# Two LoRA splits and two weight merges change places in a one-core transformer block kernel

## The chip, the cores and the metric

The kernel runs on one core of a Trainium2 chip. The metric is the device time of one execution in microseconds. A core has five engines with a queue of instructions each: TensorE (PE in the profile, with its weight loads as PEld), VectorE (DVE), ScalarE (ACT), GpSimd (POOL) and SyncE (SP, here the queue that issues nearly all DMAs). They run side by side and wait for each other through semaphores; within an engine the order is the program's.

## The reference

B = 2 batches of S = 512 rows of D = 512 features, HID = 1376, LoRA rank R = 16, all in float32.

```
mod = silu(c) @ wmod            -> sa, ca, ga, sb, cb, gb   (six rows of 512 for each batch)
ga, gb: the sign times max(|.|, 0.25)
h = layernorm(x) * (1 + ca) + sa
x = x + ga * (h @ W'^T + bias)                W' = weight, 32x32 blocks whose mask sums to 0 cleared
h = layernorm(x) * (1 + cb) + sb
h1 = h @ (w1 + 2 B1 A1)^T ;  h3 = h @ (w3 + 2 B3 A3)^T
x = x + gb * ((silu(h1) * h3) @ (w2 + 2 B2 A2)^T)
```

(The reference adds the LoRA terms as separate products; the kernel merges them into the weights.)

## The kernel before, in words

**Precision by parts.** Every float32 product is made as three products of rounded halves: high x high, high x low, low x high. So each operand needs a "high" copy (ScalarE) and a "low" remainder (VectorE or GpSimd, value minus high).

**Attention stage, up to some 48 us.** `attend(b, k, m, tiles)` (L1342) adds feature chunk k of batch b into one PSUM bank for each of four row tiles. For batch 1, tiles 2 and 3 share their banks (acc[0], acc[1]) with tiles of batch 0, so `attend(1, 0, 0, last_two)` waits until VectorE's `attn_gate(0, i)` (L995) has read the bank. Behind the gates come the residual adds `add_x1` (tiles i = 0, 1 on GpSimd, L569; 2, 3 on VectorE, L1001), the layer-norm moments `moment_f` (VectorE, L843, L845), GpSimd's `root` (L525, L528) for the reciprocal deviations, `columns_f` (TensorE L1288 transposes the modulation rows, VectorE L921, L922 takes them out), `centres`, the normed tiles (ScalarE L744, VectorE L855), and TensorE's transposes `turn(q)` (L1199). The modulation rows of the second half are `mod_rows_f` (L1281), copied by ScalarE's `mod_evacuate`, behind which ScalarE makes the fourth tile's moment.

**LoRA parts.** The LoRA matrices come in five cuts. `lora_first` (GpSimd, cuts 0 and 1) or `lora_high` (ScalarE, cuts 2 to 4) writes the high copy, and `lora_part(n)` on VectorE (L982) turns it into rows that hold high or low parts, one scalar_tensor_tensor instruction for the cut (cut 1 has 640 columns, cut 2 has 1120), counted by `parts_ready`. TensorE's merge(0) waits for two of them, GpSimd's `spread(2)` (L562) for three. `spread(j)` makes the small masked copies b13 that the merges of weight tile j multiply by.

**Weights.** The hidden dimension has 11 tiles of up to 128. Each has three pieces: (j, 0) and (j, 1) are halves of w1 and w3, (j, 2) is w2. For each piece, in this order: a DMA into one of four slots of `raw`; TensorE's `merge` (the LoRA product, L1370 for the halves, L1375 for w2); VectorE's `merge` (raw + 2 x that, L1011); ScalarE's `weight_high` (L750); VectorE's `weight_low` (L1017), which also frees the slot.

**Feed-forward stage.** 22 steps s (11 for each batch). In step s TensorE makes h1 into bank up_a, then h3 into up_b: `up_high` (high and low weights by the high activations, L1388, 8 products) and `up_rest` (high weights by the low activations, L1397, 4 products). In between it makes the merges of the next tile (`pieces_up(s)`), and behind h3 the `down` products (L1414 to L1416) of the step before. VectorE and ScalarE: Silu of up_a (L808), g = up_b x that (L1136), g_hi (L818), g_lo (L1142). Step 0 is written out by hand: high products of both banks first, then the rests, as the low activations come late, and `gate_rows(1)` (L1303) at its end, which waits for the merge whose bank it takes. The order of every queue is written by hand, in the loops over s at L802 (ScalarE), L1116 (VectorE) and L1486 (TensorE) and the straight lines ahead of them.

Of the kernel before, what the change touches and what calls it, by code (L numbers as in the profile page):

```python
# [130 lines left out]
def build(nc, x, x_cols, mask, weight, bias, ffn, lora, c, wmod_ca, wmod_sa, wmod, identity, consts, out):  # L131
# [4 lines left out]
    with ExitStack() as ctx:  # L136
# [474 lines left out]
        def _(act):  # L611
# [135 lines left out]
            def weight_high(r):  # L747
                act.wait_ge(merged, r + 1)
                src, dst, _ = weight_parts(r)
                nc.scalar.activation(dst, src, ACT.Copy).then_inc(w_high_ready, 1)  # L750
# [50 lines left out]
            lora_high(2)  # L801
            for s in range(B * HT):  # L802
                w = WIDTH[s % HT]
                act.wait_ge(h1_out, s + 1)
                if s:

                    act.wait_ge(g_low_ready, s)
                nc.scalar.activation(g[0:w], up_a[0:w], ACT.Silu).then_inc(silu_ready, 1)  # L808
                for at in pieces_up(s):
                    weight_high(PIECE[at])  # L810
                if piece_mid(s):
                    weight_high(PIECE[piece_mid(s)])
                if s == 0:
                    gate_abs(1)
                elif s == HT:
                    gated_high(0)
                act.wait_ge(g_ready, s + 1)
                nc.scalar.activation(g_hi[s % 2][0:w], g[0:w], ACT.Copy).then_inc(g_high_ready, 1)  # L818
                for j in gated_at(s):
                    gated_high(j)  # L820
                if piece_late(s):
                    weight_high(PIECE[piece_late(s)])
                if s == 0:
                    lora_high(3)
                elif s == 1:
                    lora_high(4)
                if s in STEP_TURN:
                    modulate_tile(STEP_TURN[s])

        @block.vector  # L830
        def _(dve):
# [85 lines left out]
            def columns_f():  # L917

                dve.wait_ge(cols_out, 1)
                src = up_b[:, 0:HALF].rearrange("p (c v h b) -> p v h c b", c=2, v=2, h=2)  # L920
                nc.vector.tensor_copy(shift[:].rearrange("p (h c) b -> p h c b", h=2), src[:, 0, :, :, 0:B])  # L921
                nc.vector.tensor_scalar(one_plus[:].rearrange("p (h c) b -> p h c b", h=2), src[:, 1, :, :, 0:B],  # L922
                                        1.0, None, ALU.add).then_inc(cols_ready, 1)
# [50 lines left out]
            def lora_part(n):  # L974
                lo, hi = LORA_CUTS[n]
                keep = KEEP_A if n in LORA_A else KEEP_B
                if n < LORA_POOL:
                    dve.wait_ge(parts_high_by_pool, n + 1)
                else:
                    dve.wait_ge(parts_high_ready, n + 1 - LORA_POOL)  # L980
                dve.wait_ge(const_loaded, 16)
                nc.vector.scalar_tensor_tensor(parts[:, lo:hi], f32(parts[:, lo:hi]), const[:, keep:keep + 1],  # L982
                                               lora_place(n), ALU.mult, ALU.add).then_inc(parts_ready, 1)
# [97 lines left out]
            uv_split()  # L1081
            masked_weight_low(1, 3)
            x_low(1, 3)
            lora_part(1)

            dve.wait_ge(norm_rows_out, 1)
            nc.vector.memset(f32(norm_values(0)), 0.0).then_inc(norm_first_cleared, 1)
# [4 lines left out]
            def moment_f(i):  # L1092
                dve.wait_ge(*x1_done(i))
                moment(NORM_F[0], i, xt[:, 0, ORDER[i]])
# [3 lines left out]
            add_x1(0, 3)  # L1098
            moment_f(1)
            moment_f(2)  # L1100
            columns_f()
            centres()
            norm_parts(1)
# [6 lines left out]
            for q in range(KT):  # L1110
                if q in WHOLE_DVE:
                    whole(q)
                low(q)
            lora_part(2)
            attn_gate(1, 0)
            for s in range(B * HT):  # L1116
                w = WIDTH[s % HT]
                if s == 5:
                    for t in range(2, T):
                        norm(1, t, t)  # L1120
                for at in pieces_up(s):
                    merge(PIECE[at])
                if s == 1:
                    lora_part(3)
                for at in pieces_up(s):
                    weight_low(PIECE[at])
                if piece_mid(s):
                    merge(PIECE[piece_mid(s)])
                    lora_part(4)
                    weight_low(PIECE[piece_mid(s)])  # L1130
                if s == HT:
                    gate_weights(0)

                dve.wait_ge(silu_ready, s + 1)
                dve.wait_ge(h3_out, s + 1)
                nc.vector.tensor_tensor(g[0:w], up_b[0:w], g[0:w], ALU.mult).then_inc(g_ready, 1)  # L1136
                if s == 0:
                    gates_of(1)
                if piece_late(s):
                    merge(PIECE[piece_late(s)])  # L1140
                dve.wait_ge(g_high_ready, s + 1)
                nc.vector.tensor_tensor(g_lo[s % 2][0:w], g[0:w], f32(g_hi[s % 2][0:w]),  # L1142
                                        ALU.subtract).then_inc(g_low_ready, 1)
                if piece_late(s):
                    weight_low(PIECE[piece_late(s)])
                if s < 2:
                    for i in ((1,), (2, 3))[s]:
                        attn_gate(1, i)
                if s == 2:
                    for i in range(T):  # L1150
                        add_x1(1, i)
                elif s in (3, 4):
                    for t in (2 * s - 6, 2 * s - 5):
                        dve.wait_ge(x1_by_dve, T - len(X1_POOL) + ORDER.index(t) + 1)
                        moment(NORM_F[1], t, xt[:, 1, t])
                    if s == 4:
                        for t in range(2):
                            norm(1, t, t)
                if s == HT:
                    gated_low(0)  # L1160
                    for n in range(T):
                        down_end(n)
                for j in gated_at(s):
                    gate_weights(j)
                    gated_low(j)
# [4 lines left out]
        def _(pe):  # L1170
# [114 lines left out]
            def columns_f():  # L1285
                pe.wait_ge(mod_rows_ready, 1)
                for c in range(2):
                    last = nc.tensor.transpose(up_b[:, c * P:(c + 1) * P], mod_rows[:, c * P:(c + 1) * P], ident[:])  # L1288
                last.then_inc(cols_out, 1)
# [101 lines left out]
            def up_rest(s, n, dst, signal):  # L1391
                b, j = divmod(s, HT)
                w = WIDTH[j]
                for k in range(KT):
                    if s == 0:
                        pe.wait_ge(low_by_dve, k + 1)
                    last = nc.tensor.matmul(dst[0:w], up_hi[j][:, k, n], ht_lo[b][:, k],  # L1397
                                            start=False, stop=(k == KT - 1))
                last.then_inc(signal, 1)
# [71 lines left out]
                attend(1, 1, m, last_two)  # L1471
            attend(1, 2, 0, last_two)
            columns_f()
            pe.wait_ge(parts_ready, 2)
            merge(0)
            for m in range(1, 3):
                attend(1, 2, m, last_two)
            attend(1, 3, 0, last_two)
            merge(1)
            attend(1, 3, 1, last_two)  # L1480
# [5 lines left out]
            for s in range(B * HT):  # L1486
                if s == HT:

                    pe.wait_ge(high_ready, KT + T)
                    pe.wait_ge(low_by_pool, T)  # L1490

                pe.wait_ge(*((silu_ready, s) if s else h_done(0)))
                if s:
                    up(s, 0, up_a, h1_out)
                else:

                    up_high(0, 0, up_a)

                    pe.wait_ge(*h_done(1))
                    up_high(0, 1, up_b)  # L1500
                    up_rest(0, 0, up_a, h1_out)
                for at in pieces_up(s):
                    merge(PIECE[at])
                if s == 2:

                    for t in range(T):
                        down(0, t)
                    merge(PIECE[piece_mid(s)])
                if s:

                    pe.wait_ge(g_ready, s)
                    up(s, 1, up_b, h3_out)
                else:
                    up_rest(0, 1, up_b, h3_out)
                if s == 0:
                    gate_rows(1)
                elif s == 1:
                    merge(PIECE[piece_late(s)])
                else:
                    for t in range(T):  # L1520
                        down(s - 1, t)
                        if t == 1 and piece_late(s):
                            merge(PIECE[piece_late(s)])
                if s in STEP_TURN:
                    turn_tile(STEP_TURN[s])
# [87 lines left out]
```

## Time and profile before

| | |
|---|---|
| median of 3 runs | 248.74 us (248.71 to 249.12) |
| the profiled execution's own time | 248.83 us |
| its span, first to last instruction | 247.0 us |
| busy: TensorE, its weight loads | 239.6 us (97%), 186.9 us (76%) |
| busy: VectorE, ScalarE, GpSimd | 150.1 (61%), 93.8 (38%), 41.9 us (17%) |
| granted TensorE clock | 0.999 of full speed |
| DMA | 26.38 MB, some 400 GB/s from 6 to 43 us, little after |

Times are from the start of the span. An engine's row gives the start and length of an instruction, or of several alike in one row (x4); the next instruction of VectorE starts some 0.08 us before the end of the one ahead of it, so what an instruction costs its queue is the distance of two starts. TensorE's products overlap more: one of 128x512 shows 0.39 us and is followed by the next after about 0.23. "[0.73 <-DVE wa L995]" is idle time ahead of the row and what ended it. A share of busy time says little here: it is an average over a first stage in which all engines have work and a second one in which TensorE is nearly alone.

### The profile page before, as it was taken

Reading aid. Unit: us, or ns where it says so; the run is one execution under the profiler, and the core shown is the slowest. Engines: PE = TensorE matmul, PEld = TensorE weight load, DVE = VectorE, ACT = ScalarE, POOL = GpSimd, SP = SyncE. Lnnn points to the kernel's source line nnn. Section 1 sums busy time; section 2 is a strip of 40 time slices with the busy share of each in tenths; the row PEclk is TensorE's granted clock in tenths of the full one; section 3 lists DMA queues with packets and bytes.
Section 4 is the critical chain, followed back from the end, with each engine's and each line's share of the span. In section 5 each row is a group of like instructions: output and inputs, shape, how many; then the busy total and the mean of one; then the engine's idle time right before and its main releaser. Section 6 shows DMA issues by size and latency. Waiting matters only on the chain.

```text
span 247.0 us, 3419 instructions
## 1 busy us (share of the span) xinstructions
PE 239.6 (97%) x1201; PEld 186.9 (76%) x1201; DVE 150.1 (61%) x262; ACT 93.8 (38%) x173; POOL 41.9 (17%) x57
## 2 busy tenths in 40 slices
PE   7999989999999999999999999999999999999993
PEld 5567556677778888888888778888888888888772
DVE  2779798989979768755555514745354245424524
ACT  2364495957443231647456212113121212122210
POOL 2002686311101034033032000440000000000000
PEclk9999999999999999999999999999999999999999
DMA  5999999702331231331234650030000000000005
GB/s 139 339 399 390 387 406 391 200 24 85 106 134 60 87 127 44 98 115 44 89 101 80 42 37 0 25 145 3 0 1 0 0 3 0 0 0 0 3 0 170
DMA packets 14565, 26.38 MB, mean 107 GB/s; under 512 B 1618, under 2 KB 3538, under 8 KB 14420
## 3 DMA queue, kind: packets, MB, share of 16 engines
q1 hardware_dynamic: 14112, 26.01, 34.5%
q8 instruction: 10, 0.16, 0.3%
q10 hardware_dynamic: 436, 0.15, 0.2%
q14 instruction: 7, 0.06, 0.1%
HBM read 23.27 MB, written 2.10 MB: 103 GB/s over the span
## 4 chain that ended last, share of the span: by engine, by line
PE 84%; DVE 7%; DMA 2%; issue 2%; ACT 2%; POOL 1%; SPq 0%; DVEq 0%; POOLq 0%; ACTq 0%
PE up_a L1388 17%; PE up_b L1388 16%; PE acc L1414 8%; PE up_a L1397 8%; PE acc L1416 8%; PE acc L1415 8%; PE up_b L1397 8%; PE acc L1342 3%; DMA wa<-in_weight 2%; PE side L1370 2%; PE side L1342 2%; DVE wa_lo L944 1%; DVE xt L1041 1%; DVE stats L843 1%; PE side L1375 1%
## 5 line engine op out<-in xcount | busy, mean ns | idle before, releaser
L1136 DVE TENSOR_TENSOR g<-up_b,g 128x512 f32<-128x512 f32 (+1 forms) x22 | 15.2, 690 | 43.2 <-PE up_b L1397 43.2
L1414 PE MATMUL acc<-w_hi,g_hi 128*128 128x512 f32 (+1 forms) x88 | 35.0, 397 | 0.0
L1416 PE MATMUL acc<-w_hi,g_lo 128*128 128x512 f32 (+1 forms) x88 | 34.8, 395 | 0.0
L1415 PE MATMUL acc<-w_lo,g_hi 128*128 128x512 f32 (+1 forms) x88 | 34.8, 395 | 0.0
L818 ACT ACTIVATE g_hi<-g 128x512 fp32r<-128x512 f32 (+1 forms) x22 | 13.9, 632 | 51.6 <-DVE g L1136 51.6
L1011 DVE SCALAR_TENSOR_TENSOR raw<-side,raw 128x512 f32<-128x512 f32 (+2 forms) x31 | 20.2, 677 | 19.1 <-PE side L1370 11.4
L750 ACT ACTIVATE w_hi<-raw 128x512 fp32r<-128x512 f32 (+2 forms) x33 | 20.3, 626 | 17.1 <-DVE raw L1011 17.0
L808 ACT ACTIVATE g<-up_a 128x512 f32<-128x512 f32 (+1 forms) x22 | 13.1, 596 | 32.6 <-PE up_a L1397 32.6
L1388 PE MATMUL up_a<-ht_hi,w_hi 128*128 128x512 f32 (+1 forms) x88 | 24.7, 401 | 0.3 <-ACT w_hi L750 0.3
L1388 PE MATMUL up_b<-ht_hi,w_hi 128*128 128x512 f32 (+1 forms) x88 | 23.9, 393 | 0.0
L1397 PE MATMUL up_b<-ht_lo,w_hi 128*128 128x512 f32 (+1 forms) x88 | 23.8, 392 | 0.0
L1397 PE MATMUL up_a<-ht_lo,w_hi 128*128 128x512 f32 (+1 forms) x88 | 23.8, 392 | 0.0
L1388 PE MATMUL up_a<-ht_hi,w_lo 128*128 128x512 f32 (+1 forms) x88 | 23.8, 392 | 0.0
L1388 PE MATMUL up_b<-ht_hi,w_lo 128*128 128x512 f32 (+1 forms) x88 | 23.7, 391 | 0.0
L1017 DVE TENSOR_TENSOR w_lo<-raw,w_hi 128x512 fp32r<-128x512 f32 (+2 forms) x33 | 21.6, 680 | 1.8
L1142 DVE TENSOR_TENSOR g_lo<-g,g_hi 128x512 fp32r<-128x512 f32 (+1 forms) x22 | 15.1, 688 | 8.1 <-ACT g_hi L818 7.9
L1414 PEld LDWEIGHTS acc<-w_hi,g_hi 128*128 128x128 f32 (+1 forms) x88 | 16.6, 188 | 4.4 <-issue 0.6
L562 POOL TENSOR_SCALAR b<-parts,half_on 128x128 fp32r<-128x128 f32 (+1 forms) x22 | 14.7, 678 | 29.9 <-PE side L1370 29.2
L1416 PEld LDWEIGHTS acc<-w_hi,g_lo 128*128 128x128 f32 (+1 forms) x88 | 16.6, 188 | 4.0
L1415 PEld LDWEIGHTS acc<-w_lo,g_hi 128*128 128x128 f32 (+1 forms) x88 | 16.6, 188 | 3.8
L1388 PEld LDWEIGHTS up_a<-ht_hi,w_lo 128*128 128x128 f32 (+1 forms) x88 | 16.3, 186 | 4.1
L1388 PEld LDWEIGHTS up_a<-ht_hi,w_hi 128*128 128x128 f32 (+1 forms) x88 | 15.9, 186 | 4.5 <-issue 0.5
(167 smaller groups left out, 340.8 us busy)
## 6 DMA issues: line engine op xcount, KB each, us to landing
raw<-in_ffn SPq DMA_DIRECT2D x33, 256.0 KB, 2.6
xt<-in_x SPq DMA_DIRECT2D x8, 256.0 KB, 10.8
wmod_sb<-in_wmod SPq DMA_DIRECT2D x2, 1024.0 KB, 15.3
wmod_sb<-in_wmod SPq DMA_DIRECT2D x1, 2048.0 KB, 14.5
out<-xt SPq DMA_DIRECT2D x8, 256.0 KB, 2.5
mask_sb<-in_mask SPq DMA_DIRECT2D x4, 256.0 KB, 7.1
ca_sb<-in_wmod_ca SPq DMA_DIRECT2D x4, 256.0 KB, 6.5
wa<-in_weight SPq DMA_DIRECT2D x4, 256.0 KB, 7.3
```

The source lines that it names most:

```text
L562: nc.gpsimd.tensor_scalar(b13[:, n, 0:w], f32(parts[:, LORA_B13 + j * P:LORA_B13 + j * P + w]), half_on[:, n:n + 1], None, ALU.mult).then_ ...
L750: nc.scalar.activation(dst, src, ACT.Copy).then_inc(w_high_ready, 1)
L818: nc.scalar.activation(g_hi[s % 2][0:w], g[0:w], ACT.Copy).then_inc(g_high_ready, 1)
L1011: nc.vector.scalar_tensor_tensor(w, merge_bank(r)[0:rows, 0:cols], SCALING, w, ALU.mult, ALU.add).then_inc(merged, 1)
L1017: nc.vector.tensor_tensor(low_part, src, f32(high), ALU.subtract).then_inc(w_ready, 1)
L1136: nc.vector.tensor_tensor(g[0:w], up_b[0:w], g[0:w], ALU.mult).then_inc(g_ready, 1)
L1142: nc.vector.tensor_tensor(g_lo[s % 2][0:w], g[0:w], f32(g_hi[s % 2][0:w]), ALU.subtract).then_inc(g_low_ready, 1)
L1388: nc.tensor.matmul(dst[0:w], w_part[j][:, k, n], ht_hi[b][:, k], start=(m == 0 and k == 0), stop=False)
L1397: last = nc.tensor.matmul(dst[0:w], up_hi[j][:, k, n], ht_lo[b][:, k], start=False, stop=(k == KT - 1))
L1414: nc.tensor.matmul(acc[t][:], hi, down_hi[j][0:w], start=(j == 0), stop=False)
L1415: nc.tensor.matmul(acc[t][:], hi, down_lo[j][0:w], start=False, stop=False)
L1416: last = nc.tensor.matmul(acc[t][:], lo, down_hi[j][0:w], start=False, stop=(j == HT - 1))
```

## The change

On VectorE, lora_part(1) moves from ahead of the four gates of batch 0 to behind the third tile's moments. lora_part(2) moves from behind the low activations to behind the merges of step 0, ahead of the low parts of the same pieces. On ScalarE the high part of piece (1, 0) is made ahead of step 0's Silu. On TensorE four attention products move ahead of merge(0) and its wait, and the merges of weight tile 1 move ahead of the rest of h1 in step 0. No instruction is added or removed.

```diff
@@ ScalarE, step loop
             for s in range(B * HT):
                 w = WIDTH[s % HT]
+                if s == 0:
+
+                    weight_high(PIECE[1, 0])
                 act.wait_ge(h1_out, s + 1)
...
                 for at in pieces_up(s):
-                    weight_high(PIECE[at])
+                    if at != (1, 0):
+                        weight_high(PIECE[at])
@@ VectorE
             masked_weight_low(1, 3)
             x_low(1, 3)
-            lora_part(1)
 
             dve.wait_ge(norm_rows_out, 1)
...
             moment_f(1)
             moment_f(2)
+            lora_part(1)
             columns_f()
...
                 low(q)
-            lora_part(2)
             attn_gate(1, 0)
             for s in range(B * HT):
...
                 for at in pieces_up(s):
                     merge(PIECE[at])
-                if s == 1:
-                    lora_part(3)
+                if s < 2:
+                    lora_part(2 + s)
                 for at in pieces_up(s):
                     weight_low(PIECE[at])
@@ TensorE
             columns_f()
+            for m in range(1, 3):
+                attend(1, 2, m, last_two)
             pe.wait_ge(parts_ready, 2)
             merge(0)
-            for m in range(1, 3):
-                attend(1, 2, m, last_two)
             attend(1, 3, 0, last_two)
...
                     pe.wait_ge(*h_done(1))
                     up_high(0, 1, up_b)
-                    up_rest(0, 0, up_a, h1_out)
                 for at in pieces_up(s):
                     merge(PIECE[at])
+                if s == 0:
+                    up_rest(0, 0, up_a, h1_out)
```

## Rows read from the trace of the kernel before

**Rows 1.** The page, section 4: shares of the chain that ended last, by engine.

```profile
PE 84%; DVE 7%; DMA 2%; issue 2%; ACT 2%; POOL 1%; SPq 0%; DVEq 0%; POOLq 0%; ACTq 0%
```

**Rows 2.** Table of stretches: from:to us, length, busy us (instructions) of each engine.

```profile
65.00:100.00 35.00, 34.97 (x159) 28.45 (x158) 28.90 (x50) 12.31 (x21) 7.22 (x12) 1.00 0.29 91
```

**Rows 3.** Timeline of TensorE, 34 to 67 us: start, length, what [idle before].

```profile
34.71 0.62 PE L1342 MATMUL acc<-wa_hi,ht_lo 128*128 128x512 f32 x2
36.07 1.06 PE L1342 MATMUL acc<-wa_hi,ht_hi 128*128 128x512 f32 x2 [0.73 <-DVE wa L995]
...
53.49 0.63 PE L1370 MATMUL side<-b,parts 128*128 128x256 f32 x4
...
55.23 1.08 PE L1303 MATMUL side<-wmod_sb,silu_c 128*32 128x128 f32 x32 [0.17 <-DVE raw L1011]
56.58 1.17 PE L1388 MATMUL up_a<-ht_hi,w_hi 128*128 128x512 f32 x4 [0.27 <-ACT w_hi L750]
...
59.42 0.64 PE L1370 MATMUL side<-b,parts 128*128 128x256 f32 x4
...
66.31 0.48 PE L1414 MATMUL acc<-w_hi,g_hi 128*128 128x512 f32 x1
```

**Rows 4.** Timeline of VectorE, 34 to 45 us.

```profile
34.34 0.90 DVE L982 SCALAR_TENSOR_TENSOR parts<-parts,const,lora_raw 128x640 fp32r<-128x640 f32 x1
35.20 1.37 DVE L995 SCALAR_TENSOR_TENSOR wa<-acc,rstd,mask_sb 128x512 f32<-128x512 f32 x2
...
37.82 1.28 DVE L1001 TENSOR_TENSOR xt<-wa,xt 128x512 f32<-128x512 f32 x1
...
39.83 0.66 DVE L1001 TENSOR_TENSOR xt<-wa,xt 128x512 f32<-128x512 f32 x1
...
42.71 0.17 DVE L921 COPY shift<-up_b 128x8 f32<-128x8 f32 x1 [0.59 <-PE up_b L1288]
...
43.63 0.68 DVE L1011 SCALAR_TENSOR_TENSOR raw<-up_a,raw 128x512 f32<-128x512 f32 x1
44.44 1.06 DVE L855 TENSOR_SCALAR work<-xt,moments,rstd 128x512 f32<-128x512 f32 x2
```

**Rows 5.** Timeline of GpSimd, 33 to 56 us.

```profile
33.45 2.27 POOL L562 TENSOR_SCALAR b<-parts,half_on 128x128 fp32r<-128x128 f32 x2 [0.40 <-PE up_b L1315]
36.01 2.54 POOL L569 TENSOR_TENSOR xt<-wa,xt 128x512 f32<-128x512 f32 x2 [0.29 <-DVE wa L995]
...
41.87 0.71 POOL L528 TENSOR_TENSOR rstd<-rstd,exponent 128x2 f32<-128x2 f32 x1
...
43.69 0.71 POOL L528 TENSOR_TENSOR rstd<-rstd,exponent 128x2 f32<-128x2 f32 x1
...
54.32 1.18 POOL L562 TENSOR_SCALAR b<-parts,half_on 128x128 fp32r<-128x128 f32 x2 [8.09 <-PE side L1370]
```

**Rows 6.** Timeline of VectorE, 51 to 67 us.

```profile
51.57 0.69 DVE L886 TENSOR_TENSOR ht_lo<-hbuf,ht_hi 128x512 fp32r<-128x512 f32 x1 [0.37 <-ACT hbuf L723]
52.53 1.38 DVE L982 SCALAR_TENSOR_TENSOR parts<-parts,const,ca_sb 128x1120 fp32r<-128x1120 f32 x1 [0.27 <-ACT parts L759]
...
54.49 1.28 DVE L1011 SCALAR_TENSOR_TENSOR raw<-side,raw 128x512 f32<-128x512 f32 x2
55.87 1.29 DVE L1017 TENSOR_TENSOR w_lo<-raw,w_hi 128x512 fp32r<-128x512 f32 x2
57.08 0.68 DVE L1136 TENSOR_TENSOR g<-up_b,g 128x512 f32<-128x512 f32 x1
...
59.93 1.29 DVE L1011 SCALAR_TENSOR_TENSOR raw<-side,raw 128x512 f32<-128x512 f32 x2
...
65.52 0.68 DVE L1017 TENSOR_TENSOR w_lo<-raw,w_hi 128x512 fp32r<-128x512 f32 x1
```

**Rows 7.** Timeline of ScalarE, 55 to 57 us.

```profile
55.21 1.23 ACT L750 ACTIVATE w_hi<-raw 128x512 fp32r<-128x512 f32 x2 [0.92 <-DVE raw L1011]
```

**Rows 8.** DMA issues at 23.2 us: out<-in, count, KB, us from issue to landing.

```profile
wmod_sb<-in_wmod SPq DMA_DIRECT2D x1, 2048.0 KB, 14.5
```

## The prediction

> **What bounds the kernel now.** The chain of waits comes first: 84% of the span on it is TensorE, 7% VectorE [rows 1]. The table of stretches then says where TensorE can still gain: from 65 to 100 us it works 34.97 of 35.00 us [rows 2], and it stays as dense to the end, so nothing behind 65 us gives anything by itself, while each microsecond by which TensorE reaches that point earlier comes off the end. So I read the timeline of each engine from 33 to 67 us. TensorE is held there in four places that bear on the change. Ahead of 36.07 us it waits for VectorE's first attention gate; issue stood at 34.71 + 2 x 0.237 = 35.18 [rows 3] (0.237 us is the pace of one product of 512 columns: twelve lie between 56.58 and 59.42). At 45 us its transposes wait for the two normed tiles that VectorE starts at 44.44 [rows 4]. Ahead of the gate rows at 55.23 it waits for a merge on VectorE, ahead of 56.58 for ScalarE's high part of the second weight tile [rows 3]: the four merge products of 53.49 and the four of the rest behind them would be issued by 54.91, so 0.3 us are lost there, and about 0.3 us again behind the gate rows. VectorE itself is full from 43.63 to 66 us, with gaps of 0.37, 0.27 and less [rows 4, 6], so both engines have to come earlier, or one holds the other.
>
> **First part: lora_part(1) behind the moments.** At 34.34 VectorE starts lora_part(1), and at 35.20 the memset and gate 0: 0.86 us in front of the gates [rows 4]. What else the gates need (the last attention products, the copy of the gate row) is there by 34.3, so I take the four gates 0.86 us earlier, and TensorE's 36.07 at 35.2, directly behind its 34.71 group. TensorE's next outside limit is the 2 MB of modulation weights: issued at 23.19 and landed 14.5 us later, at 37.7 [rows 8], against a new need at about 38.0. It just fits, and another 0.1 us here would not matter, because VectorE and not TensorE sets the next step.
>
> On VectorE the 0.86 us do not all survive. The add at 37.82 takes 1.28 us where the same form at 39.83 takes 0.66; it ends 0.55 us behind GpSimd's second add, which ends at 38.55 [rows 4, 5]. So this add goes by GpSimd. GpSimd is busy until 35.72 with the two spreads at 33.45, which take 2.27 us where the pair at 54.32 takes 1.18 [rows 5]; the second of them ran beside lora_part(1). Without that neighbour I let it end at about 35.3; then the two adds of 2.54 us end at 37.9, VectorE's add at 38.45 and everything up to the third moment 0.65 us earlier than before, at 41.47. If the spread stays as long as it is, the adds end at 38.3 and only 0.26 us survive.
>
> The Trainium skill (SBUF — State Buffer, Who interferes with whom) says that VectorE and GpSimd lock one port pair for a whole instruction, and that a VectorE instruction contends with a reading GpSimd one only with two SBUF inputs. By that rule the gates (one input in PSUM) leave the spread alone, and the 1.28 us of the add are a lock, in which the trace agrees; it would give the 0.65, not the 0.26.
>
> Now lora_part(1) itself runs, from 41.39 for 0.86 us, to 42.25. Before, VectorE sat idle 0.59 us ahead of 42.71, waiting for TensorE's columns [rows 4]; these now come at 41.85. So columns_f starts at about 42.2, 0.5 us earlier: the move pays with a gap that was empty. merge(0) follows 0.92 us later (42.71 to 43.63), at 43.12. TensorE's side of it, now behind four attention products and the wait for parts, is issued at about 42.55 and usable 0.51 us later (59.42 to 59.93 in the later merge [rows 3, 6]), at 43.06: level, no new stall. The four products moved ahead cost nothing, they are the same work in another order. Then the norm starts at 43.12 + 0.61 = 43.73, if the reciprocal deviations are there: GpSimd's last root ends at 44.40 now [rows 5] and hangs on ScalarE's moment behind TensorE's modulation rows, so it comes at 43.55. Before it was 44.44. I take **0.65 us** for this part. Bounds: up, the whole 0.86. Down: with 0.26 us, the norm at 44.1, 0.3 us gained. Lower still if lora_part(1) meets GpSimd's root at 41.87 (41.2 now), 0.71 us long [rows 5], and is held to its end: together with the 0.26 that is columns_f at about 43.1, a norm at 44.65, 0.2 us lost. The nearest row speaks against: the add at 39.83 ran its plain 0.66 us beside such a root.
>
> **Second part: the merges of weight tile 1 ahead of the rests, lora_part(2) behind them.** I work in the old clock, as if the first part did nothing. TensorE removes nothing; the four products at 53.49 [rows 3] move in front of the four of the h1 rest, and are issued four products earlier (4 x 0.23), at 52.57. Their banks are free by then (ScalarE's and VectorE's reads end at 51.5). Their results are usable at 53.08. VectorE frees itself from the last low part (51.57, 0.69) at 52.18 [rows 6]. Its sequence was: 0.35 us waiting for ScalarE's copy, lora_part(2) 1.30 (52.53 to 53.83), gate 0.66, two merges 1.3, 0.09 idle, two low parts 1.21, g at 57.08 [rows 6]. Now: gate 0.66 to 52.84, 0.24 us waiting for the merge, merges 1.21 to 54.29, lora_part(2) 1.30 to 55.59, low parts 1.21 to 56.80. So g comes 0.28 us earlier. ScalarE: high part of piece (1,0) from 53.8, Silu behind it at 54.35 (its input, behind the moved merges, is ready at 54.1), high part (1,1) done at 55.5, against 56.44 now [rows 7]. TensorE: rests to 54.9, gate rows without a wait to 55.9, step 1 at 55.95 instead of 56.58. Four products later it needs the low parts: at 56.9, and they end at 56.86, so it is held 0.1 us. Its merges of step 1 come at 58.87 instead of 59.42, and VectorE, which waited some 0.2 us for them at 59.93 [rows 6], starts them at 59.44. From there to the low part at 65.52 its order is the old one, 0.49 us earlier; TensorE's down product of 66.31 follows that low part (end 66.20) within 0.1 us [rows 3, 6]. So VectorE, not the 0.63 us that TensorE has gained, sets it: **0.5 us**. Bounds: up 0.63. Down: GpSimd's next spreads (54.32, 1.18 us [rows 5]) wait for the merge and for lora_part(2), so they now start at about 55.7, beside the two low parts, instead of beside merges. One spread of 0.6 let in ahead of a low part makes it -0.1, both make it -0.7. The row at 33.45 is the nearest: there GpSimd was the one stretched, so I keep the 0.5. The same page's lock would make either engine wait here, by which comes first; VectorE's queue is the fuller one. The spreads themselves have until 58.9 before TensorE wants them, 2 us of slack. Silu behind a high part costs nothing, as g waits for VectorE anyway. No DMA moves: the weight loads hang on the low parts, all earlier or at most as late.
>
> **Sum.** 0.65 + 0.50 = 1.15 us off the profiled execution's own 248.83 (span 247.03 and 1.8 around it), which is 0.09 above the median 248.74: 247.7 us. All that is gained at 66 us is carried, as TensorE does not wait behind it.
>
> **Rivals.**
> (a) Only the first part pays; a spread gets in between VectorE's low parts and the step-1 start is again held. For it: VectorE has no gap up to 66 us. 248.83 - 0.65 + 0.1 = 248.3.
> (b) Only the second pays; lora_part(1) meets GpSimd's root, columns_f stays at 42.7 to 43.1, the normed tiles where they were. Against: the add at 39.83. 248.83 - 0.5 + 0 to 0.2 = 248.3 to 248.5.
> (c) Neither: 248.8. The move of lora_part(2) only swaps one VectorE item for another, which is true of its sum; what counts is 0.28 us of idle time and the 0.2 at 59.93.
> (d) Slower: both spreads win against both low parts. They then end at 56.86 + 1.2 = 58.1, where TensorE wants them at 56.9 and had them in time for 57.59 before; 0.7 us lost there. With the first part at -0.2 to 0.3 this is 249.1 to 249.7. It decides from 0.55 us of hold on: below that the second part still gains. A pair of spreads did once take 2.27 us, but VectorE's own instructions around it were not longer.
>
> **Numbers.** Forecast (own range 247.2 to 248.2) 0.55; (a) 0.16; (b) 0.13; (c) 0.08; (d) 0.08. What a measurement can tell is about 0.5 us, so faster means below 248.24. Faster: 0.55 and half of (a) and a third of (b), some 0.68. Slower: (d), 0.08, of which a little stays within; with a little for what I don't see 0.08. Same: 0.24. The range reaches from both upper bounds (0.86 + 0.63, 247.3) and some slack, 247.1, to 248.7, and leaves out (c) and (d).
>
> **What would show it.** Gate 0 at about 34.4 and no idle time of TensorE ahead of its product behind it; the first add on VectorE ending at 38.5; lora_part(1) without idle time behind it, columns_f at 42.2; the first transpose 0.65 us earlier than 45.56. Then gate rows with no wait, step 1 at some 55.3 (56.58 - 0.65 - 0.6), the low parts of tile 1 at their 0.69 us each, the first down product at 65.2. Wrong if a low part of tile 1 or lora_part(1) is over 1.2 us long, if TensorE idles ahead of the modulation rows at 38, or if the lead at 56 is gone by 66.

## The result and the profile after

The changed kernel takes 248.10 us (median of 8 runs, 247.80 to 248.43), the kernel before 248.94 (8 runs, 248.71 to 249.72): the ratio is 0.9963, 95% interval 0.9953 to 0.9973, that is 0.92 us less (0.67 to 1.17), where 1.15 was forecast. (The medians themselves differ by 0.84. The forecast time was 247.7: of the 0.4 us between it and 248.10, 0.2 are the median of the kernel before, which was 248.74 over its first three runs and 248.94 over eight.) The profiled execution took 248.22 us, with a span of 246.4.

The timeline of TensorE in the changed kernel (start, length, what; all line numbers behind the change are some 3 to 4 higher than before):

```profile
34.37 0.50 PE L1354 MATMUL side<-uv_parts,norm_rows 12*128 12x512 f32 x2
...
35.85 1.07 PE L1345 MATMUL acc<-wa_hi,ht_hi 128*128 128x512 f32 x2
...
43.23 0.41 PE L1373 MATMUL up_a<-b,parts 128*128 128x256 f32 x2
...
45.45 0.66 PE L1202 MATMUL up_a<-ident,work 128*128 128x128 f32 x4 [0.21 <-DVE work L859]
...
48.49 1.40 PE L1391 MATMUL up_a<-ht_hi,w_hi 128*128 128x512 f32 x4
...
52.48 0.64 PE L1373 MATMUL side<-b,parts 128*128 128x256 f32 x4
...
54.89 1.08 PE L1306 MATMUL side<-wmod_sb,silu_c 128*32 128x128 f32 x32
55.90 1.20 PE L1391 MATMUL up_a<-ht_hi,w_hi 128*128 128x512 f32 x4
...
65.72 0.47 PE L1417 MATMUL acc<-w_hi,g_hi 128*128 128x512 f32 x1
```

Three of the stalls of [rows 3] are gone: 35.85 has no idle time ahead of it, neither have the gate rows (54.89) and step 1 (55.90). The first down product comes at 65.72 instead of 66.31, and from there both kernels take the same 180.7 us to the end. VectorE in the same kernel:

```profile
34.10 0.69 DVE L901 TENSOR_TENSOR ht_lo<-raw,ht_hi 128x512 fp32r<-128x512 f32 x1
...
34.95 1.41 DVE L999 SCALAR_TENSOR_TENSOR wa<-acc,rstd,mask_sb 128x512 f32<-128x512 f32 x2
...
37.60 1.31 DVE L1005 TENSOR_TENSOR xt<-wa,xt 128x512 f32<-128x512 f32 x1
...
41.86 0.86 DVE L986 SCALAR_TENSOR_TENSOR parts<-parts,const,lora_raw 128x640 fp32r<-128x640 f32 x1
42.64 0.16 DVE L925 COPY shift<-up_b 128x8 f32<-128x8 f32 x1
...
43.74 0.69 DVE L1015 SCALAR_TENSOR_TENSOR raw<-up_a,raw 128x512 f32<-128x512 f32 x1
...
52.99 1.29 DVE L1015 SCALAR_TENSOR_TENSOR raw<-side,raw 128x512 f32<-128x512 f32 x2 [0.16 <-PE side L1373]
54.19 1.38 DVE L986 SCALAR_TENSOR_TENSOR parts<-parts,const,ca_sb 128x1120 fp32r<-128x1120 f32 x1
55.48 1.29 DVE L1021 TENSOR_TENSOR w_lo<-raw,w_hi 128x512 fp32r<-128x512 f32 x2
56.69 0.69 DVE L1139 TENSOR_TENSOR g<-up_b,g 128x512 f32<-128x512 f32 x1
```

The 0.59 us of idle time of [rows 4] is filled by lora_part(1), at 41.86. But the absolute times at 45 us puzzle: the first transposes come at 45.45 against 45.56. The reader must not compare clocks that started apart. One of VectorE's moments for batch 0 (BATCH_NORM_STATS2 of its second row tile, an instruction ahead of all that was changed; the expectations below call it the first moment of the batch, but one at 21.94 us stands ahead of it) began at 24.22 us in the profile before and at 24.68 in this one, without any change to what stands ahead of it. So all profiles below are cut at four instructions that every kernel has: that moment, the last attention products of batch 0 (at 34.36 here), the first up product (48.49) and the first down product (65.72). Each column is the distance of two starts, in us, read from the timelines:

| kernel | moment to last products | last products to gate 0 | moment to first up | first up to first down |
|---|---|---|---|---|
| before | 9.48 | 1.50 | 24.37 | 17.72 |
| before, second and third profile | 9.88, 9.48 | 1.17, 1.51 | 24.42, 24.37 | 17.69, 17.72 |
| changed | 9.68 | 0.59 | 23.81 | 17.23 |
| changed, second profile | 9.70 | 0.59 | 23.79 | 17.26 |
| first part alone | 9.85 | 0.59 | 23.96 | 17.73 |
| second part alone | 9.50 | 1.50 | 24.39 | 17.23 |
| lora_part(1) alone | 9.89 | 0.59 | 24.06 | 17.98 |
| changed, lora_part(2) back | 9.49 | 0.67 | 23.64 | 18.13 |
| changed, moment first | 9.83 | 0.59 | 23.92 | 17.25 |
| changed, gates early | 9.91 | 0.59 | 24.02 | 17.18 |
| changed, all three | 9.74 | 0.59 | 23.74 | 17.17 |
| before, short copies | 9.49 | 1.17 | 24.03 | 17.72 |
| changed, short copies | 9.49 | 0.59 | 23.59 | 17.24 |

### The profile page after: what moved, and what is told of

Read it like the earlier page. It is cut to its first block, busy times and chain, and to the rows that moved or that the text cites. A ratio compares the mean times of both kernels' runs of the same rounds, so it can differ in the third digit from the quotient of the medians.

```text
span 246.4 us, 3419 instructions
## 1 busy us (share of the span) xinstructions
PE 240.3 (98%) x1201; PEld 187.7 (76%) x1201; DVE 149.9 (61%) x262; ACT 93.4 (38%) x173; POOL 41.7 (17%) x57
## 4 chain that ended last, share of the span: by engine, by line
PE 87%; DVE 9%; issue 1%; POOL 1%; ACT 1%; DVEq 0%; POOLq 0%; ACTq 0%
PE up_a L1391 17%; PE up_b L1391 16%; PE acc L1417 8%; PE up_a L1400 8%; PE up_b L1400 8%; PE acc L1419 8%; PE acc L1418 8%; PE acc L1425 2%; PE acc L1345 2%; PE side L1373 2%; DVE stats L847 2%; PE side L1345 2%; DVE wa_lo L948 1%; DVE xt L1045 1%; PE side L1378 1%
## 5 line engine op out<-in xcount | busy, mean ns | idle before, releaser
L811 ACT ACTIVATE g<-up_a 128x512 f32<-128x512 f32 (+1 forms) x22 | 13.1, 595 | 31.2 <-PE up_a L1400 31.2
L1391 PEld LDWEIGHTS up_b<-ht_hi,w_lo 128*128 128x128 f32 (+1 forms) x88 | 16.3, 185 | 3.9
```

The lines of the kernel that those rows point to most:

```text
L1391: nc.tensor.matmul(dst[0:w], w_part[j][:, k, n], ht_hi[b][:, k], start=(m == 0 and k == 0), stop=False)
```

## The experiments

My theory was that the two parts add up, 0.5 us of them from the second one; the rival was that one part made all the gain.

**The first part alone** (short diff against the kernel before):

```diff
             x_low(1, 3)
-            lora_part(1)
...
             moment_f(2)
+            lora_part(1)
             columns_f()
...
+            for m in range(1, 3):
+                attend(1, 2, m, last_two)
             pe.wait_ge(parts_ready, 2)
             merge(0)
-            for m in range(1, 3):
-                attend(1, 2, m, last_two)
```

> Only the first part: lora_part(1) behind the third moment, and the four attention products ahead of merge(0). Theory (the parts add up, the profile of the changed kernel merely began 0.5 us late): 0.35 to 0.65 us faster than before. Rival (the first part gained nothing, as the absolute times at 45 us suggest: first transpose 45.45 against 45.56): 0.0 to 0.15 us faster. In the profile, counted from the last attention products of batch 0 (L1351 in the kernel before), gate 0 comes 0.9 us earlier by both, the norm at least 0.5 us earlier by the theory alone.

Measured: ratio 0.9976 (0.9962 to 0.9990), 0.60 us faster (0.25 to 0.95). From the moment to the first up product it gains 0.41 us, within the theory's 0.35 to 0.65. Counted from the last attention products, gate 0 comes 0.91 us earlier (0.59 against 1.50) and the norm 0.75. The rival's 0.0 to 0.15 is out.

**The second part alone** (all other edits of the change):

> Only the second part: lora_part(2) behind the merges of weight tile 1, these merges ahead of the rest of h1, the high part of piece (1,0) ahead of Silu. Theory: 0.5 us faster than before, g of step 0 0.3 us earlier, the first down product 0.5 us earlier, counted from the first up product. Rival (the second part made all the gain): 0.8 to 0.9 us faster.

Measured: 0.9974 (0.9961 to 0.9987), 0.65 us faster (0.32 to 0.97); 17.23 against 17.72 between first up and first down, 0.49 us, and nothing ahead of it. The time alone would leave room for the rival's 0.8 to 0.9; the profile, and the gain of the first part by itself, do not. Each part gains by itself. The sum of the two gains, 0.50%, is within the interval of the next run (0.35 to 0.77%) and a little above that of the result (0.27 to 0.47%), which the parts' own intervals of some 0.14% each allow.

**The changed kernel again**, beside the parts, no edit:

> The changed kernel again, beside the parts: 0.8 to 1.1 us faster than before by the theory that the parts add up (0.35 to 0.65 and 0.5). A second profile of it shows how far the start (the time of the last attention products of batch 0, 34.36 in the first) varies from one execution to the next: if it is 33.7 again, the first transpose should come at about 44.9.

Measured: 0.9944 (0.9923 to 0.9965), 1.4 us faster with a wide interval. The last attention products stood at 34.19, so the start did not fall back to 33.7, and the distances repeat the first profile's to 0.03 us.

**lora_part(1) alone.** TensorE keeps its old order, merge(0) and its wait ahead of the four products:

```diff
 (against the first part alone)
-            for m in range(1, 3):
-                attend(1, 2, m, last_two)
             pe.wait_ge(parts_ready, 2)
             merge(0)
+            for m in range(1, 3):
+                attend(1, 2, m, last_two)
```

> Only lora_part(1) is moved on VectorE; TensorE keeps merge(0) ahead of the four attention products. Theory: merge(0) on VectorE waits in the changed kernel for TensorE's merge (0.51 us behind its issue at 43.23), so the old order on TensorE, whose wait ends with lora_part(1) at 42.7, is as fast or up to 0.1 us faster than the first part with both edits. Rival: without the four products TensorE idles 0.3 to 0.5 us ahead of merge(0) and all of that is lost: 0.3 to 0.5 us slower than with both edits.

Measured: 0.9991 (0.9978 to 1.0005), 0.2 us faster (-0.1 to 0.5): the reorder of four products on TensorE is worth some 0.37 us, as the rival had it (0.3 to 0.5), and my theory fell. In the profiles 0.10 us of it is lost ahead of the first up product (24.06 against 23.96) and 0.25 behind it (17.98 against 17.73). Counted from the last products of batch 0 (33.80 here, 33.88 with both edits) the norm did come 0.14 us earlier (43.65 against 43.87), as it said. The loss stands one queue further, on ScalarE:

```profile
43.85 0.62 ACT L750 ACTIVATE w_hi<-raw 128x512 fp32r<-128x512 f32 x1
45.28 0.60 ACT L692 ACTIVATE norm_rows<-side 108x512 fp32r<-108x512 f32 x1 [0.82 <-PE side L1269]
45.78 0.62 ACT L750 ACTIVATE w_hi<-raw 128x512 fp32r<-128x512 f32 x1
```

With both edits the same three lines read:

```profile
43.98 0.63 ACT L750 ACTIVATE w_hi<-raw 128x512 fp32r<-128x512 f32 x1
44.79 0.60 ACT L692 ACTIVATE norm_rows<-side 108x512 fp32r<-108x512 f32 x1 [0.18 <-PE side L1269]
45.55 0.63 ACT L750 ACTIVATE w_hi<-raw 128x512 fp32r<-128x512 f32 x1 [0.15 <-DVE raw L1011]
```

TensorE idles 0.33 us ahead of merge(0), its moment transposes (L1269) come 0.57 us later by the same count (44.65 against 44.16), ScalarE's copy of them waits, and the high part behind that copy is 0.31 us late. VectorE waits for it (0.58 us ahead of its low part at 46.43) and is late for all that follows.

**lora_part(2) back.** The changed kernel with this one item where it was:

```diff
                 low(q)
+            lora_part(2)
             attn_gate(1, 0)
...
-                if s < 2:
-                    lora_part(2 + s)
+                if s == 1:
+                    lora_part(3)
```

> The changed kernel with lora_part(2) back ahead of gate (1, 0): of the second part only TensorE's merges and ScalarE's high part stay moved. Theory: VectorE's merges cannot begin before 54.4, so the early merges on TensorE find nobody, and VectorE's idle 0.35 us ahead of lora_part(2) is back: g of step 0 comes where it was before, the second part gives 0.0 to 0.25 us, the kernel is 0.5 to 0.8 us faster than before. Rival (it is TensorE's early merges and the gate rows without a wait that pay): the whole 0.5 us stays, 1.1 us faster than before.

Measured: 0.9998 (0.9988 to 1.0007): the whole gain is gone, which neither theory had. Its profiled execution, 248.60 us, is among the four shortest of its eleven (248.57 to 248.60; the others took 248.79 to 249.50), and there 0.32 us are left at the first down product, 0.73 gained ahead of the first up product and 0.41 lost behind it (18.13 against 17.72). The loss is what has to be explained. TensorE's timeline:

```profile
54.59 1.08 PE L1307 MATMUL side<-wmod_sb,silu_c 128*32 128x128 f32 x32 [0.17 <-DVE raw L1015]
56.35 0.47 PE L1392 MATMUL up_a<-ht_hi,w_hi 128*128 128x512 f32 x1 [0.68 <-ACT w_hi L750]
```

And ScalarE's:

```profile
54.57 0.63 ACT L750 ACTIVATE w_hi<-raw 128x512 fp32r<-128x512 f32 x1 [2.71 <-DVE raw L1015]
55.11 0.58 ACT L811 ACTIVATE g<-up_a 128x512 f32<-128x512 f32 x1
55.58 0.62 ACT L750 ACTIVATE w_hi<-raw 128x512 fp32r<-128x512 f32 x1
```

ScalarE's Silu (L811) now stands behind the high part of piece (1, 0), which waits for VectorE's merge at 53.86. In the kernel before, it ran at 53.69, ahead of both high parts and in idle time; here it stands between them, so the second high part and with it step 1 are late. Without the move of lora_part(2), then, ScalarE's new order turns a late VectorE merge into a stall. What TensorE's early merges would do without ScalarE's edit was not run.

**The first moment ahead of VectorE's add.**

```diff
-            add_x1(0, 2)
             moment_f(0)
+            add_x1(0, 2)
             add_x1(0, 3)
```

> The changed kernel with moment_f(0) ahead of VectorE's add_x1(0, 2), which held VectorE for 1.3 us beside GpSimd's adds. By the lock theory the add now takes 0.66 us and the third moment ends 0.6 us earlier. But the norm behind merge(0) is then set by TensorE (merge issued at 43.23, usable 0.51 us later) and GpSimd's last root (ends at 44.16 where the norm starts at 44.35), so the time is 0.0 to 0.2 us below the changed kernel's: 0.9 to 1.3 us faster than before. Rival (VectorE still sets the first transposes): all of the 0.6 us comes off, 1.6 us faster than before.

Measured: 0.9959 (0.9947 to 0.9972), 1.0 us faster than before, no more than the changed kernel. VectorE:

```profile
37.11 0.68 DVE L847 BATCH_NORM_STATS2 stats<-xt 128x6 f32<-128x512 f32 x1
37.83 0.18 DVE L849 BATCH_NORM_AGGREGATE moments<-stats 128x2 f32<-128x6 f32 x1
37.93 1.26 DVE L1005 TENSOR_TENSOR xt<-wa,xt 128x512 f32<-128x512 f32 x2
...
40.73 0.86 DVE L986 SCALAR_TENSOR_TENSOR parts<-parts,const,lora_raw 128x640 fp32r<-128x640 f32 x1
42.01 0.17 DVE L925 COPY shift<-up_b 128x8 f32<-128x8 f32 x1 [0.42 <-PE up_b L1291]
```

Two adds now take 1.26 us where one took 1.31. So the long add was a wait for GpSimd's adds. The Trainium skill (SBUF — State Buffer, Who interferes with whom) has it as a lock between GpSimd and a VectorE instruction with two SBUF inputs (the prediction said "only"; the page names VectorE's two-port modes as a second case, which no run here shows); the moment, with one input, ran beside the same GpSimd add in its plain 0.68. And the 0.6 us won turn into idle time ahead of columns_f (0.42 us, for TensorE's up_b): behind the changed kernel's first part, TensorE and no longer VectorE sets this place. The theory's 0.9 to 1.3 us holds, the rival's 1.6 is out.

**The gates early**, in VectorE's gap ahead of the last low activation:

```diff
+                if q == 3:
+                    attn_gate(1, 0)
+                    attn_gate(1, 1)
                 low(q)
-            attn_gate(1, 0)
...
-                    for i in ((1,), (2, 3))[s]:
+                    for i in ((), (2, 3))[s]:
```

> The changed kernel with VectorE's gates (1, 0) and (1, 1) ahead of the last low activation, where VectorE idles 0.38 us, and gate (1, 1) gone from between g_lo and the merges of step 1. Theory: VectorE and not TensorE sets the first down product. The low activation comes 0.9 us later (TensorE wants it at 53.7, it has 0.6 us), the merges of tile 1 0.1 us later, the low part in front of the down product 0.1 to 0.3 us earlier: 0.1 to 0.2 us below the changed kernel's time. Rival (TensorE sets it): nothing or up to 0.2 us lost.

Measured: 0.9960 (0.9947 to 0.9974), the changed kernel's time. First up to first down gains 0.05 us, 17.18 against 17.23, and VectorE shows where the gate's 0.66 us went:

```profile
58.30 0.69 DVE L1147 TENSOR_TENSOR g_lo<-g,g_hi 128x512 fp32r<-128x512 f32 x1 [0.18 <-ACT g_hi L822]
59.49 0.69 DVE L1015 SCALAR_TENSOR_TENSOR raw<-side,raw 128x512 f32<-128x512 f32 x1 [0.50 <-PE side L1375]
```

It waits 0.50 us for TensorE's merge: in the changed kernel both are due there within 0.1 us of each other (VectorE starts the merge at 59.34, TensorE's product of 58.77 is usable at 59.28), so the rival was nearer.

**All three**: both edits above, and merge(0) between the four products:

```diff
-            for m in range(1, 3):
-                attend(1, 2, m, last_two)
+            attend(1, 2, 1, last_two)
             pe.wait_ge(parts_ready, 2)
             merge(0)
+            attend(1, 2, 2, last_two)
```

> The changed kernel with the edits of the two kernels above and merge(0) on TensorE between the attention products (1, 2, 1) and (1, 2, 2). Theory: merge(0) is usable 0.45 us earlier, the norm then waits for GpSimd's root and starts 0.15 to 0.2 us earlier; with the early gates 0.2 to 0.4 us below the changed kernel's time, 1.1 to 1.6 us faster than before. Rival (what is gained ahead of the transposes is eaten on ScalarE's queue, where the copy of the norm rows stands ahead of the high part of piece 1): no more than the early gates give alone.

Measured: 0.9955 (0.9943 to 0.9968), 247.67 us, not told apart from the changed kernel (0.9963 and 0.9944). The distances, 23.74 and 17.17, put it 0.1 us ahead, short of the theory's 0.2 to 0.4. Counted from the last attention products, VectorE's merge(0) came 0.14 us earlier than in the changed kernel (9.24 against 9.38), the norm 0.15 (9.84 against 9.99) and the first up product 0.13 (14.00 against 14.13): to move merge(0) on TensorE moves all three.

**The copies cut short.** What stayed open was why the first part gained 0.35 to 0.58 us in four profiles (moment to first up, against 24.37: both of the changed kernel, the first part alone, the gates early), and 0.73 in one, the kernel with lora_part(2) back. GpSimd's LoRA copies run beside VectorE's gate signs (L969) and gate split (L975) there. In the changed kernel, with TensorE's transposes that wait for the gate signs:

```profile
29.91 2.77 POOL L540 TENSOR_SCALAR parts<-lora_raw 128x256 fp32r<-128x256 f32 x2 [0.71 <-DVE norm_cols L884]
...
31.88 0.62 PE L1272 MATMUL up_b<-ident,norm_cols 128*108 128x128 f32 x4 [0.29 <-DVE block_ones L969]
...
31.25 0.48 DVE L969 SCALAR_TENSOR_TENSOR block_ones<-mod_rows,block_ones 128x128 f32<-128x128 f32 x1
32.11 0.35 DVE L975 SCALAR_TENSOR_TENSOR b<-b,const,block_ones 128x128 fp32r<-128x128 f32 x1 [0.38 <-ACT b L708]
```

In the kernel with lora_part(2) back, where GpSimd's copy started 0.5 us later behind the moment:

```profile
30.10 3.05 POOL L540 TENSOR_SCALAR parts<-lora_raw 128x256 fp32r<-128x256 f32 x2 [1.26 <-DMA lora_raw<-in_lora]
...
30.88 0.29 DVE L969 SCALAR_TENSOR_TENSOR block_ones<-mod_rows,block_ones 128x128 f32<-128x128 f32 x1
31.55 0.65 DVE L975 SCALAR_TENSOR_TENSOR b<-b,const,block_ones 128x128 fp32r<-128x128 f32 x1 [0.38 <-ACT b L708]
```

One of the two is stretched, by which of them meets the copy, and the same holds in every other profile with the copies whole. When it is the gate signs, TensorE's transposes wait for them (0.29 us idle above), and so the last attention products come late; when it is the gate split, they don't. Two kernels cut the copies to 2 columns (the LoRA part of cuts 0 and 1 is then left out of the result):

```diff
-                nc.gpsimd.tensor_scalar(parts[:, lo:hi], lora_place(n), 1.0, None, ALU.mult
+                nc.gpsimd.tensor_scalar(parts[:, lo:lo + 2], lora_place(n)[:, 0:2], 1.0, None, ALU.mult
```

> The kernel before, with GpSimd's two copies of LoRA cuts 0 and 1 cut to 2 columns each (the rest of the high copy is 0, set at the start, so this LoRA part is left out of the result). These copies ran from 29.9 to 33.1 us beside VectorE's gate signs and splits, and in most profiles of the changed kernel one of these VectorE instructions took 0.5 us instead of 0.3. Theory (that stretch is a collision, whose outcome differs from one execution to the next): no VectorE instruction between 30 and 33 us is stretched, the last attention products of batch 0 start at most 9.5 us after VectorE's first moment of the batch (24.22 to 33.70 in the kernel before), and the time is 0 to 0.4 us below before. Rival (it has another cause): the stretch stays.

> The changed kernel with the same two copies cut to 2 columns (the same LoRA part is left out). Theory: from the first moment to the last attention products it takes as long as in its partner, and the two parts then add up undisturbed, 0.65 to 0.8 us up to the first up product and 0.5 us behind it: 1.1 to 1.3 us below its partner. Rival (the change itself costs time ahead of the gates): the stretch of 0.2 to 0.4 us stays in this kernel alone, and it is 0.8 to 0.95 us below its partner.

Measured: 0.9986 (0.9977 to 0.9996) and 0.9953 (0.9939 to 0.9966). Without the copies both instructions are plain in both kernels (0.29 and 0.35), and both take 9.49 us to the last products: the stretch is a collision with the copies, shown. The gap between the two is 0.33%, 0.8 us, in one pair of profiles 0.44 + 0.48 + the difference of their starts. The theory's 1.1 to 1.3 missed. The 0.8 is the size the rival gave, but not its reason, as the stretch stayed in neither. The table has the reason: in the partner gate 0 still follows VectorE (1.17 us behind the last products), in the changed one it follows the last products (0.59). So the partner gains by an unstretched gate split, 0.34 us up to the first up product (24.37 to 24.03), where the changed kernel gains only 0.05 against its best profile (23.64 to 23.59). Of the 0.73 us in that profile, then, some 0.3 are a stretched gate split that no longer holds up the gates, and 0.44 remain where there is no collision at all.

**Two more profiles of the kernel before**, no edit:

> The kernel before once more, for a second profile of it. Open is whether the stretched gate signs on VectorE (0.5 us instead of 0.3 ahead of 31.3 us, GpSimd's LoRA copy starting 5.2 to 5.6 us behind the first moment instead of 5.7 to 5.8) belong to the moved kernels or come and go with the execution. If they come and go, one of two further profiles of the kernel before shows them, with the last attention products of batch 0 some 9.7 to 9.9 us behind the first moment instead of 9.5; if they belong to the change, neither does. The time itself is that of before, within 0.1%.

> A third profile of the kernel before, to the same end: 9.5 us from the first moment to the last attention products if the stretch belongs to the change, 9.7 to 9.9 in one of the two if it comes and goes.

Measured: 0.9999 (0.9988 to 1.0010), and 249.18 us in the single run. The second profile has the late outcome (9.88 us), the first and third have the other (9.48, with the gate split 0.65 us long). In the second:

```profile
29.96 0.86 DVE L897 TENSOR_TENSOR ht_lo<-raw,ht_hi 128x512 fp32r<-128x512 f32 x1
...
31.05 0.52 DVE L965 SCALAR_TENSOR_TENSOR block_ones<-mod_rows,block_ones 128x128 f32<-128x128 f32 x1
```

Two instructions are stretched here, the low activation from 0.68 us and the gate signs from 0.29; 0.18 and 0.23 us are just what the last products are late by (0.40), and with the gate signs alone, as in the changed kernel, it is 0.20. So the late outcome comes and goes with the execution. And which of the two outcomes it is costs the kernel before next to nothing, 24.42 against 24.37, as lora_part(1) kept gate 0 back anyway. One thing stays open: one of four profiles with lora_part(1) in its old place had the late outcome, and seven of eight with it moved. VectorE's and GpSimd's order up to there is the same, and so few profiles do not show whether the moved kernels meet it more often.

## Why the prediction was right, and where it was off

**The second part** was right step by step. Forecast 0.5 us, measured 0.49 in the profiles (17.72 to 17.23) and 0.65 (0.32 to 0.97) by time. In the kernel with this part alone, whose clock agrees with that of before, g of step 0 starts at 56.80 (56.80 forecast), VectorE's merges of step 1 at 59.45 (59.44), the first down product at 65.82 (66.31 less 0.49). That the lead of TensorE (0.57 us at step 1) shrinks to VectorE's 0.49 by the down product was the point on which the size hung. The collision of rivals (a) and (d) took place and fell on the other side. In the changed kernel GpSimd's spreads took 2.08 us instead of 1.18, beside two low parts (55.48) of 1.29 us together, as before:

```profile
55.66 2.08 POOL L562 TENSOR_SCALAR b<-parts,half_on 128x128 fp32r<-128x128 f32 x2 [9.54 <-DVE parts L986]
```

The early gates add that VectorE has the smaller lead only by a hair.

**The first part** was right in kind and too large in size, 0.65 against 0.35 to 0.58 in four profiles out of five, 0.73 in the fifth. VectorE and GpSimd did what the forecast said: without lora_part(1) beside them the two spreads took 1.73 us in the changed kernel and 1.94 with lora_part(2) back, against 2.27, so the bound of 0.26 us is out. In the kernel with lora_part(2) back, set on the clock of the kernel before by the moment at 24.22, GpSimd's adds end at 37.91 (37.9 forecast), VectorE's add at 38.46 (38.45), the third moment at 41.48 (41.47), columns_f starts at 42.18 (42.2), merge(0) at 43.12 (43.12) and the norm at 43.72 (43.73). In the changed kernel, on the same clock, the third moment (41.48) and columns_f (42.18) are the same. Rival (b) is out: lora_part(1) took its plain 0.86 us although GpSimd's root ran from 41.70 to 42.41 beside it.

The step that was mis-sized is TensorE's side of merge(0): "issued at about 42.55 and usable 0.51 us later [...], at 43.06: level, no new stall". On the same clock it was issued at 42.77 in the changed kernel and usable at 43.28, so VectorE's merge came 0.35 us earlier than before instead of 0.51, and the norm 0.55 instead of 0.71. In the first part alone and the gates early the issue was at 42.93 and 42.99, and the norm came 0.38 and 0.33 us earlier. The reason is one queue: in the seven profiles that have all four products ahead of merge(0), TensorE issues merge(0) 8.86 to 8.91 us behind the last attention products, without a pause in between, and the first up product 14.09 to 14.15 us behind them.

Being level, the step had no slack, and each 0.1 us by which those products are late is lost. They are 0.2 to 0.4 us late when the gate signs meet GpSimd's copy. Before, lora_part(1) covered that. The forecast had the tie right, but took the products' time from one profile as fixed, when it was one outcome of a race: "What else the gates need (the last attention products, the copy of the gate row) is there by 34.3". Gate 0, which waits for the same products (0.59 us behind their start), was late by it too, 0.71 us gained instead of 0.86 in the changed kernel, but up to columns_f that cost nothing there, as GpSimd's adds ended where the forecast had them (37.89).

**One edit was priced wrongly at nothing**: the four attention products ahead of merge(0) ("they are the same work in another order"). They are what makes most of lora_part(1)'s move pay, 0.37 us by time, because the wait for parts would otherwise delay everything behind merge(0) in TensorE's queue. The sum was unaffected, as it was made for the edits together.

Together: 0.49 + 0.35 to 0.58 = 0.84 to 1.07 us (1.05 and 1.04 in the two profiles of the changed kernel itself), beside the result's 0.92; the forecast's 1.15 lies just within its interval.

## What to carry to other kernels

When the instruction that hides a supplier is moved away, the next supplier's spread from one execution to the next becomes the kernel's: take two or three profiles of the kernel before and use the late outcome. A step that a forecast finds "level" between two engines has no slack: ask what each of the two hangs on, and how far that varies. Compare profiles by distances between instructions that both have, not by clock times, since the same moment starts anywhere from 23.91 to 24.68 us in these profiles. And a set of moves in several queues is one edit: undoing a single one of them (lora_part(2)) lost all that the time can show, and leaving one out that looked free (four products) lost most of its half.

## What was not expected of the hardware

GpSimd's root of 1.03 us from 39.58 and VectorE's add of two SBUF inputs at 39.65 ran side by side without stretching it (0.67 us), as did lora_part(1) beside the 0.71 us root; GpSimd's instructions on 128x512 and on 128x128 did hold or were held. With the moment first, on the other hand, lora_part(1) at 40.73 came ahead of a root and stretched that from 0.71 to 1.26 us. So in these runs a GpSimd instruction on 2 or 4 columns did not hold VectorE, and one of them was held by it.
